# Reordering the first stages of a fused four-layer graph network kernel, and pairing the chunks of its sort stage

## The reference, cut to what matters

```python
edge_index = stack([src, dst])
h = maximum(_layernorm(x), 0);  x = x + rgcn(h, edge_type_3, edge_attr_32, ...)      # 3 rounds
h = maximum(_layernorm(x), 0);  x = x + gated(h, edge_attr_64, W1, b1, W2, b2, ...)
h = maximum(_layernorm(x), 0);  x = x + relational_attention(h, edge_type_8, ...)
h = maximum(_layernorm(x), 0);  x = x + distance_attention(h, edge_weight, ...)
# in rgcn, per edge:   relu(h[src] * (edge_attr_32 @ nn_w.T + nn_b)), mean by (dst, type), times W[type]
# in gated, per edge:  gate = sigmoid(silu(edge_attr_64 @ W1 + b1) @ W2 + b2);  msg = gate * h[src]
```

## Time and profile before

| what | value |
|---|---|
| runs, us | 6715.25 median of 3 (6707.17 to 6726.9) |
| the profiled execution: own time, span | 6715.85, 6713.9 |
| PE busy | 4619.3 us, 69% of the span |
| PEld, DVE, ACT, POOL busy | 57%, 47%, 45%, 51% |
| emptying, sort stage, first normalize with weight turning (from the timeline) | about 52, 716 and 72 us |

### The profile page before, as it was taken

One profiled execution on the slowest core, in us unless ns is written; L12 is line 12 of the kernel. 1 busy time (PEld: TensorE's weight loads), 2 busy tenths in 40 slices (PEclk: granted clock), 3 DMA queues, 4 the chain that ended last, 5 costly groups with the idle time before them and its releaser, 6 DMA issues. The chain is left out here.

```text
span 6713.9 us, 120607 instructions
## 1 busy us (share of the span) xinstructions
PE 4619.3 (69%) x23667; PEld 3817.1 (57%) x23668; DVE 3138.4 (47%) x8626; ACT 3008.7 (45%) x9887; POOL 3438.9 (51%) x3945
## 2 busy tenths in 40 slices
PE   3599975776766677847777545557586777557786
PEld 2488863655655566736666334456465666345564
DVE  6355544444434444434444434444424555634445
ACT  0244433555525555435555234443125555345554
POOL 0255544555465555565655655565335555235553
PEclk9799987999988888978888766667786667666666
DMA  5533334334513333323334055554243333633333
GB/s 99 110 113 111 112 88 103 99 97 98 89 42 91 92 92 92 48 76 93 94 93 68 20 158 159 164 167 90 77 133 81 80 80 81 44 91 79 78 79 76
DMA packets 590821, 627.04 MB, mean 93 GB/s; under 512 B 318127, under 2 KB 484870, under 8 KB 590726
## 3 DMA queue, kind: packets, MB, share of 16 engines
q0 software_dynamic: 163840, 423.87, 24.8%
q1 hardware_dynamic: 419350, 189.28, 12.1%
q10 hardware_dynamic: 7536, 12.91, 0.9%
HBM read 481.63 MB, written 143.24 MB: 93 GB/s over the span
## 5 line engine op out<-in xcount | busy, mean ns | idle before, releaser
L804 POOL DMA_INDIRECT G<-h_dram,idx x1872 | 1770.6, 946 | 1292.7 <-issue 426.4
L914 PEld LDWEIGHTS ps_a<-hotm,msg 128*128 128x128 f32 x5616 | 948.4, 217 | 556.2 <-ACT msg L945 200.7
L907 PE MATMUL ps_e<-nnw,attT 128*128 128x256 f32 x2808 | 986.3, 438 | 391.4 <-ACT attT L930 185.4
L914 PE MATMUL ps_a<-hotm,msg 128*128 128x128 f32 x5616 | 985.9, 304 | 375.4 <-DVE arena L976 246.8
L796 ACT ACTIVATE hotm<-dist,ones 128x128 f32<-128x128 f32 x2292 | 888.8, 388 | 356.3 <-DMA bias<-L_gnn_bias 229.8
L790 ACT ACTIVATE dist<-iota,meta 128x128 f32<-128x128 f32 x2340 | 923.4, 395 | 184.5 <-ACTq L226 112.3
L976 DVE TENSOR_TENSOR arena<-ps_a,arena 128x256 f32 x1404 | 587.8, 419 | 708.5 <-remote 334.5
L907 PEld LDWEIGHTS ps_e<-nnw,attT 128*128 128x128 f32 x2808 | 490.0, 218 | 466.6 <-ACT attT L930 218.1
L638 POOL DMA_INDIRECT rec_dram<-rec,pos x392 | 376.0, 959 | 590.1 <-issue 295.9
L1128 PE MATMUL ps_a<-hotm,msg 128*128 128x128 f32 x1872 | 404.4, 394 | 389.6 <-DVE arena L1165 197.7
L945 ACT ACTIVATE msg<-prodm 128x256 f32<-128x256 f32 x936 | 380.5, 407 | 641.8 <-remote 356.8
(11 more groups left out here) (274 smaller groups left out, 8185.8 us busy)
## 6 DMA issues: line engine op xcount, KB each, us to landing
gate<-rec_dram SPq DMA_DIRECT2D x156, 384.0 KB
G<-h_dram,idx POOLq DMA_INDIRECT x1872
rel_dram<-stage SPq DMA_DIRECT2D x25, 1040.0 KB
attT<-attT_dram SPq DMA_DIRECT2D x104, 144.0 KB
h_dram<-hs SPq DMA_DIRECT2D x100, 128.0 KB, 1.7
rec_dram<-empty SPq DMA_DIRECT2D x1, 11242.0 KB, 70.3
at<-edge_attr SPq DMA_DIRECT2D x98, 112.0 KB
att<-rec_dram SPq DMA_DIRECT2D x52, 144.0 KB
```

The costliest lines, as they stand in the source:

```text
L804: pool.indirect_dma_start(G[:, n % width, :], None, table, bass.IndirectOffsetOnAxis(ap=idx[:, which, n:n + 1], axis=0)).then_inc(sem(f"sw ...
L907: t.matmul(ps_e[s % BANKS][:], attT[:, s // HU, s % HU, :], nnw[:], start=True, stop=True).then_inc(sem("ew"), 1)
L914: last = t.matmul(ps_a[s % BANKS][:, h, :], msg[:, s % RING, h * P:(h + 1) * P], hot[:, s, :], start=True, stop=True)
```

## The change

1. The counting block no longer empties chunks. After it stands a block that is the first `normalize`, now with `empty=`: SP alone empties all 75 last chunks, in 15 turns of five, without the check of the loaded numbers; ACT issues the writes of the normalized tiles to `h_d`, each one tile behind its activation. `hs` lies in the space of `rec`. It ends when SP has issued its transfers and the tiles have landed. Then comes the weight turning, as a function `begin_rgcn`, ahead of the sort stage.
2. `meta` is no longer loaded in a normalize. In layer 0 SP first loads its first 54 chunks (`FIRST`), ACT the other 414 as its first transfer; GpSimd makes the indices for the first piece, gathers 45 chunks, makes the indices of the second and gathers the rest. ACT waits once per 18 chunks for `columns`.
3. The sort stage works on pairs of chunks: one turning of 128 by 128 (two chunks of 64 attributes), W1 laid twice, on partitions 0 to 63 and 64 to 127, and z matmuls of 64 rows each, the two chunks of a pair on the two halves, into different PSUM banks; b1 is added on ACT and VectorE (two sigmoids and two products per pair, one for each half of the features); one gate sigmoid of 512 columns per pair. One PSUM buffer for the turned attributes instead of two. Lags are 0, 1 and 2 pairs.

```diff
-                        empty_last_chunks(nc.sync, mybir.EngineType.SP, 0, 40)
-                        empty_last_chunks(nc.scalar, mybir.EngineType.Activation, 40, KD - 40)
...
+                normalize(empty=(last_chunk, empty), hs=rec[:].rearrange("p b j w -> p (b j w)")[:, 0:TG * D].rearrange("p (s d) -> p s d", s=TG))
+                begin_rgcn(nnw, attT)
...
+        def empty_last_chunks(sp, last_chunk, empty):
+            sp.wait_ge(sem("emptied"), 16 * (1 + NC2 // EMPTY2))
+            with nc.sync.Fori(0, KD // LASTS) as i:
+                _, chunks = nc.values_load_multi_w_load_instructions(
+                    last_chunk[0:1, ds(i * LASTS, LASTS)], engines=[mybir.EngineType.SP], min_val=0, max_val=NC1 - 1,
+                    skip_runtime_bounds_check_because="last_chunk is a chunk's number less one, brought to at least 0 when it is made")
+                for c in chunks:
+                    sp.dma_start(rec_d[ds(c * P, P), :], empty[:]).then_inc(sem("emptied"), 16)
...
+                            if c1 and empty:
+                                t, i, s = c1
+                                wait_ahead(act, (sem("h"), upto(t)))
+                                nc.scalar.dma_start(h_d[ds(t * P, P), :], hs[:, s, :]).then_inc(sem(f"h_out{s}"), 16)
```

ScalarE in the sort stage:

```diff
-                        for c0, c1, c3 in walk(nc.scalar, NG // 2, 0, 2, 4, width=SW):
+                        for c0, c1, c2 in walk(nc.scalar, NG // 2, 0, 1, 2, width=PAIRS):
...
+                                nc.scalar.copy(aT[:, s % 2, :], ps_t[:]).then_inc(sem("aT_sb"), 1)
...
+                                for h in range(DH):
+                                    last = nc.scalar.activation(sig[:, s % 2, h, :, :], ps_z[s % 2][:, :, h * P:(h + 1) * P],
+                                                                ACT.Sigmoid, bias=b1[:, h:h + 1])
...
+                                nc.scalar.activation(rec[:, s // 2, at:at + 2, 0:D], ps_g[s % 2][:], ACT.Sigmoid).then_inc(sem("gate"), 1)
```

TensorE in the sort stage (behind z stand L562's matmuls in even turns and L568's in odd ones, then the pair's two times three matmuls with W2 and b2):

```diff
-                        for c0, c1, c3 in walk(nc.tensor, NG // 2, 0, 1, 4, width=SW):
+                        for c0, c1, c2 in walk(nc.tensor, NG // 2, 0, 1, 2, width=PAIRS):
...
+                                t.transpose(ps_t[:], at64[:, b, at:at + 2, :].rearrange("p c w -> p (c w)"), ident[:]).then_inc(sem("aT"), 1)
...
+                                for h in range(DH):
+                                    for j in range(2):
+                                        rows = slice(j * A64, (j + 1) * A64)
+                                        last = t.matmul(ps_z[s % 2][:, j, h * P:(h + 1) * P], W1[rows, h * P:(h + 1) * P],
+                                                        aT[rows, s % 2, :], start=True, stop=True)
+                                last.then_inc(sem("z"), 1)
```

VectorE in the sort stage:

```diff
+                                for h in range(DH):
+                                    last = v.scalar_tensor_tensor(silu[:, s % 2, h, :, :], ps_z[s % 2][:, :, h * P:(h + 1) * P],
+                                                                  b1[:, h:h + 1], sig[:, s % 2, h, :, :], ALU.add, ALU.mult)
```

Layer 0:

```diff
+                                if l == 0:
+                                    sp.dma_start(meta[:, 0:FIRST, :], meta_rows[:, 0:FIRST, :]).then_inc(sem("meta_in0"), 16)
                                 sp.dma_start(W[:], L0_gnn_W[l].rearrange("r (h p) d -> p r h d", p=P)).then_inc(sem("w_in"), 16)
...
+                                    columns_of(pool, 0, FIRST, "meta_in0")
+                                    gather_rows(pool, (0, FIRST - HU), h_d, 0, G, "prod")
+                                    columns_of(pool, FIRST, NC1, "meta_in1")
+                                    gather_rows(pool, (FIRST - HU, NC1), h_d, 0, G, "prod")
...
+                                if l == 0:
+                                    nc.scalar.dma_start(meta[:, FIRST:NC1, :], meta_rows[:, FIRST:NC1, :]).then_inc(sem("meta_in1"), 16)
...
+                                            if s == 0:
+                                                act.wait_ge(sem("columns"), i + 1)
```

More of the change, by code:

```diff
@@ L226, in credit, with sort_edges @@
                 eng.sem_inc(sem(name), CREDIT)
-        def sort_edges():
+        def sort_edges(nnw, attT):
             ctx = ExitStack()
@@ L540, in _ @@
+                            if c0 and c0[2] % 2 == 1:
+                                n, i, s = c0
+                                b = s // 2
+                                if not isinstance(i, int):
+                                    for j in range(SG):
+                                        act.wait_ge(sem(f"sw_rec{b * SG + j}"), i * OUTS)
+                                nc.scalar.copy(rec[:, b, :, WA32:WA32 + A32], at32[:, b, :, :]).then_inc(sem("a32"), 1)
                     @block.tensor
@@ L633, in _ @@
                                 for j in range(SG):
-                                    waits = [(sem("gate"), upto(g * SG + j))]
+                                    waits = [(sem("gate"), upto(g * 2 + j // 2))]
                                     if j == 0:
@@ L679, in normalize @@
+        def normalize(keep=False, empty=None, hs=None, early=()):
             ctx = ExitStack()
@@ L800, in gather_rows @@
             width = G.shape[1]
-            for n in range(chunks):
+            for n in range(*chunks):
                 if n >= width:
@@ L805, in gather_rows, with columns_of, rgcn @@
                     ap=idx[:, which, n:n + 1], axis=0)).then_inc(sem(f"sw_g{n % width}"), 16)
+        FIRST = 3 * U
+        meta_rows = rec_d[0:NC1 * P, WMETA:WMETA + NMETA].rearrange("(j p) w -> p j w", p=P)
+        def columns_of(pool, first, end, loaded):
+            pool.wait_ge(sem(loaded), 16)
+            nc.gpsimd.tensor_copy(idx[:, 0, first:end], meta[:, first:end, 1])
+            nc.gpsimd.tensor_copy(idx[:, 1, first:end], meta[:, first:end, 2]).then_inc(sem("columns"), (end - first) // U)
+            pool.wait_ge(sem("columns"), end // U)
         acc0 = arena[:].rearrange("p (b c) -> p b c", b=KD)
-        def rgcn():
+        def rgcn(nnw, attT):
             ctx = ExitStack()
             with ctx:
-                nnw_in = sb(ctx, "nnw_in", [P, DH, A32])
-                nnw = sb(ctx, "nnw", [P, D])
                 W = sb(ctx, "W", [P, R3, DH, D])
@@ L1115, in _ @@
                         def _(pool):
-                            gather_rows(pool, NC1, h_d, 0, G, "msg")
+                            gather_rows(pool, (0, NC1), h_d, 0, G, "msg")
                         @block.tensor
@@ L1832, in _ @@
                         sp.wait_ge(sem("out"), 16 * (PIECES + 1))
-        sort_edges()
-        normalize(load_meta=True)
-        rgcn()
+        with ExitStack() as ctx:
+            nnw = sb(ctx, "nnw", [P, D])
+            attT = sb(ctx, "attT", [P, 2, HU, P])
+            sort_edges(nnw, attT)
+            rgcn(nnw, attT)
         normalize(keep=True)
```

228 lines of the change are left out of this document (104 added, 124 removed).

## The result

The changed kernel takes **6683.52 us** (median of 6 runs, 6674.59 to 6705.28), the kernel before 6713.93 beside it: ratio 0.9957, 95% interval 0.9944 to 0.9969. It is faster beyond the 0.3% that can be told, but by 30 us where 82 were forecast. The profiled execution took 6679.46 us, with a span of 6677.6.

What follows compares the result with a forecast made beforehand. The prediction took PE to bound the sort stage, with the transfers' round trip next, and full DMA engines the emptying. -72.1 + 32 - 61 + 4 + 15 = -82 us against 6715.85 gave 6634 us, range 6591 to 6695.

Steps and rivals of the forecast that it cites:

- What leaves the path: After the sort: normalize and turning, between SP's meta transfer and W's, leave the path, -72.1 us.
- Before the sort: Emptying on SP alone, normalize covered beside it, turning in the open: first turning later by +32 us, ends +25 and +51.
- the low end, +25: Before the sort: a 3.9 us turn of emptying leaves the DMA time as the bound, +25 us.
- The sort stage: Paired chunks, z halves side by side with a mode-change drain: 7.07 to 6.45 us a group, -61 us.
- Rival A: Sort stage: z passes one behind another without drain, 6.69 us a group, -37 instead of -61, total 6658; chance 0.27.
- lies just under PE's time in each case: Sort stage: records' round trip through gate, transfers, places and keys takes 6.1 us a group, or 6.4 with serial z.
- of the silu chain ... a whole turn is left as slack: Sort stage: two sigmoids and two products, some 2.2 us, have a whole turn to spare.
- Layer 0: Loading meta in two pieces there: +4 us (0 to 8) for delayed attributes, +15 for ACT's stuck queue.
- Covered by VectorE's memset: Layer 0: first gather about 13 us in, hidden by a memset ending 20.3 us in; attributes landing at 24 cost +4.
- 4 to 26: Layer 0: ACT's first attribute write stalls 4 to 26 us behind meta's second piece, taken as +15.
- The 65 us of pieces that take turns with the rest: Layer 0: piece two ends 65 us in if sharing engines by turns, 43 if it fills gaps.
- Sum: Whole kernel: all terms together -82 us, 6634 us, 1.2% faster.

Runs made afterwards that it cites:

- A: Chip of the first measurement: kernel before 6713.9 us, changed kernel 6683.5 us, ratio 0.9957.
- C: Another chip: kernel before 5689.5 us, the unaltered changed kernel run again 5614.3 us, ratio 0.9862.
- z_full: Changed kernel with z in four passes over the whole array, weights padded with zeros: 5641.5 us on B, ratio 0.9923.
- D: Another chip: kernel before 6790.7 us, changed kernel 6799.8 us (ratio 1.0004), with places behind the next keys 6812.2 us (1.0032).
- E: Another chip: kernel before 6786.5 us; paired sort stage alone 6809.9 us (ratio 1.0027), new order alone 6769.6 us (0.9969).
- F: Another chip: kernel before 6723.2 us; only two variants of the changed kernel ran there, 6686.0 and 6686.1 us.
- B: Another chip: kernel before 5683.6 us; the unaltered changed kernel did not run there, only its halves and variants.
- the two halves of the change: Kernel before with only the paired sort stage, 5637.0 us; changed kernel without it, only the new order, 5673.6 us; both on B.
- places_late: Changed kernel with VectorE making a group's places behind the next group's keys and look-up: 5617.6 us on B, ratio 0.9879.

## Why the prediction was wrong

**What leaves the path** (-72.1): right. From the last record transfer to W's issue are 10.85 us, before 82.6: -71.8 on A and on C.

**Before the sort** (+32): mis-sized, first turning is +24.5 on A and +23.8 on C. 75 issues from 205.4 to 271.2 make 4.4 us a turn of five, not 5.4, so the low end, +25, was the true one. Normalize lay under it entirely, and turning's loads did queue behind SP's last transfers: TensorE's next work starts at 284.8, 79 us after the first issue, which is the prediction's figure for the transfers themselves.

**The sort stage** (-61): TensorE's side is right. 6.35 to 6.4 us a group where the stage is fast, 6.45 forecast; on C the stage is 627.4 us, -63.7 against the earlier trace rows. Rival A's serial figure, 6.69, stands in `z_full` as 6.65. The Trainium skill, TensorEngine Tiling (Array Packing), Key Properties, says that tiles work in parallel and that a change of mode drains; the trace agrees, with passes that start in pairs and two changes that cost 0.30 us a pair together where 0.32 was taken.
What failed on A is the other sentence of the step: that the other loop "lies just under PE's time in each case", and "of the silu chain ... a whole turn is left as slack". The first takes from the earlier trace rows that a gate starts 0.2 us after its matmuls, which is 0.31 after the b2 product's start; the second leaves out that the look-up stands behind silu on VectorE, and the sigmoid behind the gate on ScalarE. In the slow stretches the gate started 1.55 us after its product, and the chain from gate to gate took 7.14 us a group: gate 607.81, sigmoid 608.65, silu 609.53, look-up 610.33, counts 610.95, product 613.23, gate 614.95. The records' way is late from the same gate on: its transfers start at 609.18 and 610.44, the places follow at 613.32, the keys at 614.25, and the other counts at 614.95 after a wait of 0.69. With the places out of the way the stage was no faster on D, so the records' loop, on which the prediction set its bound, need not close for this. 21 slow turns of 48, at some 1.6 us each, are the 34 us between -61 and -27. The rows of the sort stage could not have given the lateness: with TensorE busy for 682.5 of 691 us, before has 2 late gates in 390, by 0.62 and 0.85 us from the product. But the same trace shows late copies in layer 0, where TensorE does wait, and the prediction did not look there.

**Layer 0** (+4 and +15): +23.6 on A, +31.9 on the fast chips. "Covered by VectorE's memset" failed: the first turning of attributes came 26 us behind W's issue (24 forecast), because SP stood still for 12.8 us at W's issue, behind piece one, and issued them 15 us later than before; the first message came 8 us late. The stall of the first attribute write is 7.6 us on A and 25.4 on C, inside 4 to 26; on both the queue is free 60.7 us after piece two's issue, and ScalarE only reached it later on A. The 65 us of pieces that take turns with the rest was the nearer end, not 43; the Trainium skill, DMA: Bandwidth & Descriptors, Queues, rings and completion order, has the queues take turns by packet; the trace shows that they share the engines (q10 at 61% and q0 at 43% of their time in the same 40 us), not in what steps.

**Sum** at layer 1's start on A: -71.8 + 24.5 + 3.1 (from first turning to first transfer) - 27.4 + 23.6 = -48, against -82. By far the largest miss is the sort term on a chip with late signals. On C the change brings 75 us, 1.4%. That this is near 82 is in part luck: the sort term is as forecast there and 8 us are gained before the stage, but layer 0 costs 32 where 19 were forecast.

Open stays what makes TensorE's signals late on A, D, E and F and not on B and C, and what delays turns 15, 28 and 41. The link from late gates to slow turns is read from timelines; no run could take the lateness away alone. On B the two halves of the change give 47 and 10 us, and `places_late`, the whole change with 5 us less in the stage, gives 66, so the parts nearly add up on one chip (57 and some 61); why the whole gives 75 on C stays open, since no trace of before exists on any chip but A.

## What to carry to other kernels

Before shortening the bound, lengthen each step from the bounding engine to its consumers by what the same trace shows in a stage where that engine waits, and see whether the side loops still close in time; queues served in order (gate, copy, sigmoid on ScalarE, look-up and keys behind silu on VectorE) hand one late signal on to work that does not need it. Where a software gather paces a stage, every us by which its first gather is held is paid, whatever covers the other engines' start. A gain of about 1% measured on one chip need not have the same sign on the next.

## What was not expected of the hardware

- The same kernel takes 5684 to 5690 us on two chips and 6714 to 6791 on four, with equal durations of single instructions (a record transfer's issue 0.958 us, the gate 0.60) and granted clocks that differ less than the times (0.79 to 0.81 against 0.85 to 0.87 over the span, 1.00 in the sort stage of chips A, C and D alike).
- On the slow ones the semaphore of a finished matmul may rise late: in the sort stage of A 1.58 us after the matmul's start in the median of the late cases, instead of 0.29, for one of a group's two gates inside the slow stretches and for none in the fast ones. On B and C it was never late, though TensorE waits there too.
- A whole-array matmul beside half-array ones: 0.21 us from turning to z's first pass where 0.11 is the whole-array step.
